# Graph build on one NeuronCore: waits for copies at every second step, four dump slots, and a bank-opening product with 32 rows of weights

## The reference

```python
edge_index = jnp.stack([src, dst])
h = jnp.maximum(_layernorm(x, axis=-1), 0.0)
x = x + _L0_gnn_ref(h, edge_index, edge_attr_16, ...)   # scores q.k * sigmoid(sum of attributes), mean over a target's edges
...
x = x + _L1_gnn_ref(h, edge_index, L1_gnn_W_rel, ...)   # agg = segment_sum(x[src], dst)
...
x = x + _L2_gnn_ref(h, edge_index, edge_weight, ...)    # two layers: segment_sum(x[src] * ew[:, None], dst)
...
x = x + _L3_gnn_ref(h, edge_index, edge_weight, ...)    # four heads, softmax over a target's edges
return x
```

## Time and profile before

| | |
|---|---|
| median of 3 | 8103.16 us (8084.32 to 8224.06) |
| profiled execution | 8091.68 us, its span 8089.9 us |
| mean granted TensorE clock | 0.847 over the span |
| PE busy, share of the span | 5318.0 us, 66% |
| PE weight load | 4663.3 us, 58% |
| DVE | 3863.3 us, 48% |
| ACT | 2333.4 us, 29% |
| POOL | 1739.8 us, 22% |

### The profile page before, as it was taken

The page is one execution under the profiler, slowest core; times in us unless marked ns, Lnnn a source line. Parts: engine busy times, 40 slices in busy tenths (PEclk is TensorE's granted clock), DMA queues, the critical chain, the costliest instruction groups (busy, mean ns, idle before and its releaser), DMA issues.

```text
span 8089.9 us, 151519 instructions
## 1 busy us (share of the span) xinstructions
PE 5318.0 (66%) x44994; PEld 4663.3 (58%) x44994; DVE 3863.3 (48%) x6044; ACT 2333.4 (29%) x6489; POOL 1739.8 (22%) x1693
## 2 busy tenths in 40 slices
PE   2888888888888999999999996000114531533255
PEld 2666666666667999999999995000013421432245
DVE  7999999988884222111111113000214731833478
ACT  3887777777773111110000002000000000000005
POOL 1000000000000000000000002766777266165330
PEclk9999999999999999999999996555556865866688
DMA  4345555566666666666676662333445554555465
GB/s 133 128 177 197 207 220 229 233 237 234 238 242 277 261 261 267 277 275 276 275 277 277 278 278 54 102 96 102 125 126 174 142 157 120 135 168 137 120 181 157
DMA packets 509526, 1587.66 MB, mean 196 GB/s; under 512 B 167402, under 2 KB 195148, under 8 KB 482319
## 3 DMA queue, kind: packets, MB, share of 16 engines
q1 hardware_dynamic: 425422, 1351.59, 45.5%
q0 software_dynamic: 55376, 121.59, 6.3%
q10 hardware_dynamic: 28298, 109.21, 3.6%
HBM read 972.87 MB, written 609.23 MB: 196 GB/s over the span
## 4 chain that ended last, share of the span: by engine, by line
PE 54%; issue 20%; another core or an unknown queue 9%; DVE 8%; ACT 4%; ACTq 2%; DVEq 1%; DMA 1%; SPq 0%; POOL 0%; POOLq 0%
PE psum L1079 27%; PE psum L1045 10%; PE psum L1049 9%; ACT arena L861 3%; PE psum L1207 3%; DVE arena L1830 2%; DVE arena L1840 1%; PE psum L1039 1%; ACTq L861 1%; ACTq L837 1%; DVE arena L1827 1%; DVE quad_place L1823 1%; DVEq L1840 0%; PE psum L1145 0%
## 5 line engine op out<-in xcount | busy, mean ns | idle before, releaser
L1079 PE MATMUL psum<-arena,H 128*128 128x128 f32 x19208 | 2252.8, 277 | 14.6 <-issue 14.6
L1079 PEld LDWEIGHTS psum<-arena,H 128*128 128x128 f32 x19208 | 2230.1, 188 | 14.8 <-issue 14.8
L861 ACT COPY arena<-psum x4704 | 1857.6, 410 | 504.3 <-PE psum L1049 383.8
L735 POOL DMA_INDIRECT H<-head_table,H x1568 | 1575.6, 1005 | 1138.4 <-issue 537.2
L1207 PE MATMUL psum<-arena 128*128 128x132 f32 x5088 | 871.2, 325 | 1287.3 <-issue 525.7
L1207 PEld LDWEIGHTS psum<-arena 128*128 128x128 f32 x5088 | 745.0, 223 | 1412.9 <-issue 807.4
L1039 PE MATMUL psum<-zero_b 128*128 128x2 bf16 x4704 | 789.1, 168 | 375.5 <-ACT arena L861 364.5
L1049 PE MATMUL psum<-arena 128*128 128x200 bf16 x4704 | 815.9, 255 | 0.0
L1039 PEld LDWEIGHTS psum<-zero_b 128*128 128x128 bf16 x4704 | 457.0, 97 | 614.6 <-issue 526.7
L1049 PE MATMUL psum<-H,arena 128*128 128x200 bf16 x4704 | 807.7, 253 | 0.0
L1476 DVE TENSOR_TENSOR H<-H,work 128x9408 bf16<-128x9408 bf16 x147 | 742.6, 5052 | 0.0
(11 more groups left out here) (291 smaller groups left out, 4089.4 us busy)
## 6 DMA issues: line engine op xcount, KB each, us to landing
arena<-adj SPq DMA_DIRECT2D x196, 3200.0 KB, 10.0
adj<-arena SPq DMA_DIRECT2D x1176, 400.0 KB
arena<-edge_rows SPq DMA_DIRECT2D x636, 272.0 KB
edge_rows<-H ACTq DMA_DIRECT2D x196, 544.0 KB
H<-head_table,H POOLq DMA_INDIRECT x1568
arena<-in_edge_attr SPq DMA_DIRECT2D x4, 3072.0 KB, 15.6
quad_rec<-edge_records SPq DMA_DIRECT2D x636, 10.0 KB
head_table<-arena SPq DMA_DIRECT2D x7, 476.0 KB
```

What stands on the lines that cost most here:

```text
L735: pool.indirect_dma_start(out=rows[:, j, :], out_offset=None, in_=head_table, in_offset=bass.IndirectOffsetOnAxis(ap=idx_stage[:, j:j + 1] ...
L861: act.copy(evac[:, :, bass.ds(place, SEG)], banks[:, bass.ds(bank, NSEG * SEG)].rearrange("p (w c) -> p w c", w=NSEG)).then_inc(pair_copie ...
L1079: mm = pe.matmul(ps_y[slot][:, 0:D], source[:, hi, :], adj_in[slot][:, :, 2 * hi:2 * hi + 2], start=(hi == 0), stop=(hi == NB - 1))
```

## The change

Three edits in the build, and the moves of buffers that one of them needs:

- `DUMPS` goes from 2 to 4. `evac` grows by two slots in each of three parts (600 elements per partition). To make room, the second `place_hot` buffer moves from `arena` to `work`, and `tab_rest` from `work` to `small`.
- ACT waits for `pair_copied` at even steps only, for copies up to j-3 (before: at each step, up to j-2). PE waits for `pair_copied` at even steps only, for copies up to j-4 (before: at each step, up to j-5).
- The product that opens a bank reads 32 rows of `zero_b` as weights and as moving operand, where it read 128. The one ahead of the loop (line 1028) keeps 128.

```diff
-DUMPS = 2
+ZROWS = 32
+DUMPS = 4
...
-        place_hot = [piece(BATCH * P // 2).bitcast(BF16).rearrange("p (h c i) -> p h c i", h=PACK, i=2) for _ in range(2)]
+        hots = [piece(BATCH * P // 2)]
         piece = carve(work[:, :, :].rearrange("p i f -> p (i f)"))
+        hots.append(piece(BATCH * P // 2))
+        place_hot = [t.bitcast(BF16).rearrange("p (h c i) -> p h c i", h=PACK, i=2) for t in hots]
...
-        tab_rest = piece(2 * P).rearrange("p (k s) -> p k s", k=2)
+        tab_rest = small[:, :, :].rearrange("p i f -> p (i f)")[:, 0:2 * P].rearrange("p (k s) -> p k s", k=2)
...
                 act.wait_ge(step_added, j + ADDED0)
-                act.wait_ge(pair_copied, j + 1 - DUMPS + COPIED0)
+                if j % 2 == 0:
+                    act.wait_ge(pair_copied, j + 2 - DUMPS + COPIED0)
...
-                if j >= BANKS - 3:
-                    pe.wait_ge(pair_copied, j - (BANKS - 3) + COPIED0)
-                pe.matmul(banks[:, bass.ds(after, 2)], zero_b[:, :], zero_b[:, 0:2], start=True, stop=True,
+                if j >= BANKS - 3 and j % 2 == 0:
+                    pe.wait_ge(pair_copied, j - (BANKS - 4) + COPIED0)
+                pe.matmul(banks[:, bass.ds(after, 2)], zero_b[0:ZROWS, :], zero_b[0:ZROWS, 0:2], start=True, stop=True,
                           skip_group_check=True)
```

## The result

The changed kernel takes 8439.05 us, the median of six executions (8354.5 to 8452.12), against 8175.84 us for the kernel before, measured beside it (six executions, 8084.32 to 8224.06). The ratio is 1.036, with a 95% interval of 1.028 to 1.044: slower by 3.6%, where 2.4% faster was forecast. The time lies above the predicted range of 7870 to 8300 us too.

What follows compares the result with a forecast made beforehand. ACT was taken to bound the build at 8.08 us per round; falling to 7.43 over 294 rounds saves 191 us, so about 7912 us against 8103.2, 2.4% less. The range was 7870 to 8300 us.

Steps and rivals of the forecast that it cites:

- the term of the narrow product: PE's 32-row product in each build step: bounds 0 to 0.3 us extra per step, taken as 0.
- d: Extra PE time per step from the 32-row product; PE's batch is 6.45 + 16 d us, harmless up to 0.06.
- rival A: Narrow product empties PE's pipe: 8330 us with one tail, 9035 with both; chance 0.2 of slower by over 2%.
- ACT's waits and the slots: ACT's copies in the build: 0.41 to 0.363 us each, saving 0.70 us per round of 16 steps.
- The hold on the pair of copies: ACT: copy j waits for copy j-2, so two copies cost about 0.8 us, 0.41 each.
- What is late next: DVE at 7.32 us per round, level with ACT, plus 0.11 for varying loads: 7.43 us per round.
- PE's waits: PE needs one copy more at even steps: taken as nothing; if the cover were gone, 0.34 us per round.
- The buffers that move: Buffers moved to make room for the slots: same memory, same instructions, cost nothing.
- DVE's floor of 7.32: DVE's batch in the build without its wait for PE, 7.32 us per round; alone it would give 7880 us.

## Why the prediction was wrong

**The step that failed** is the term of the narrow product: "The lower bound is 0. The upper bound is ... together 0.3 us per step. ... I take 0, because the four products of different widths now follow each other at the distance of their columns". That reason says nothing about shapes: every row of the kernel before has the shape of 128 rows. Measured is d = 0.18 us per step, in the upper half of the bounds, 0.09 ahead and 0.09 behind; alone it makes the round 8.63 us instead of 8.08. With bounds of 0 and 0.3 and no row to choose between them, nothing spoke for zero; half of the upper bound, 0.15, would have given rival A's 8330 us. By the rule of the Trainium skill, TensorEngine Tiling (Array Packing), Key Properties, a change of the tiling mode drains TensorE; the traces agree that a change costs, as products of 32 and of 64 rows pay and one of 96, which I take to have the shape of 128, doesn't.

**Rival A** was the mechanism; it had a chance of 0.2. Its formula, 6.45 + 16 d, gives 9.33 us for d = 0.18; measured is 9.03, and 8.63 with the narrow product alone. How near 9.03 comes to 9.33 is partly luck. The formula counts PE's load on top of the steps, and that was wrong: the step across the load, from one zero product to the next, took 1.35 us on average before, and 0.61 in the changed kernel (both at full clock), so the load is nearly hidden. And it has no term for the half clock, which makes up for much of it. The measured round of the changed kernel adds up as 16 x 0.52 = 8.4 for the steps, 0.15 for waits for copies (44.7 / 294), and about 0.27 for the half clock: 229 us in which a third fewer products run (297 in 60 us against 600 in 80 us), 75 to 80 us over 294 rounds. That leaves 0.2. About 0.07 of it is in the 69 steps at full clock into which PE's products for the next tables fall (lines 1007 and 1014), 0.23 and 0.35 us more each; the rest is spread over the round and not taken apart.

**ACT's waits and the slots** were right, in size too: 0.363 us per copy was taken, and 0.363 measured. A separate wait instruction costs about 0.05, as taken (0.403 to 0.349). The hold on the pair of copies, though, was the smaller part of it: the slots alone take 0.41 to 0.39.

**What is late next** was right: 7.43 us per round was forecast without a price for the product, and 7.43 measured with 128 rows; DVE's wait for PE fell to 0.13 per batch. The forecast, 7912 of 8103 us, is a ratio of 0.976; that kernel's is 0.979 (0.965 to 0.992).

**PE's waits** were right only with 128 rows: there the part does nothing (ratio 0.999). With the narrow product I had no thought of it: the cover of that step, PE's room, was gone, and one step less of lead then costs 0.45 us per round (8.58 to 9.03), more than the 0.34 named. Some 0.27 of it is the half clock, 0.11 the longer waits (44.7 instead of 11.5 us). So this term, put at nothing, failed as well. Without it the round of 8.58 us would be 8103 + 294 x 0.50 = 8250 us by the prediction's own sum, an estimate inside its range (8323 us if counted from the 8175.84 measured here).

**The buffers that move** cost nothing that shows: with them and 128 rows the round is 7.39 to 7.43, near DVE's floor of 7.32. No run moves them alone.

## What to carry to other kernels

Look at the shape of each product on TensorE and not only at its size: a product over 64 or 32 rows between products over 128 saves nothing here and costs 0.18 us each time, even with two columns. Where a copy waits for the copy two back, and semaphore and sequencer follow its end, two more buffers and a wait at every second step are worth more than the engine's busy time shows (0.41 to 0.363 us per copy, 2.6% of this kernel). A term whose bounds lie on both sides of the verdict is the prediction; when no row decides it, don't put it at nothing but take the middle and say so. A wait that costs nothing on an engine with room has to be priced again for each case in which that room is gone.

## What the runs showed that I had not expected

The clock of TensorE can stay at its lower level while PE is busy without a pause: 60.00 of 60.00 us at a granted clock of 0.50, in steps of 0.81 us, in a stretch of 79 us. The longest, with two narrow products, lasts 294 us. In the kernel before, the same engine with shorter steps and longer pauses keeps 0.98. A smaller lead of PE over ACT, worth nothing by itself, decided whether that happened at all with products of 32 or 64 rows (mean clock 0.93 to 0.97 with it, five traces; 1.00 without, three).

The register load at every 16th step differs from one to the next by a factor of more than four (541 to 2423 ns for line 840); I haven't found what decides it.
